# One burst on TensorE for the head outputs of a group, in place of two

## The reference, cut to what matters

```python
q, k, v = x @ Wq + bq, x @ Wk + bk, x @ Wv + bv      # per head, [8, 16, 512, 16]
scores = q @ k^T * 16 ** -0.5
probs = softmax(scores + causal mask)
y = probs @ v                                         # [8, 16, 512, 16]
x = layernorm(x + y @ Wo + bo)
f = silu(x @ fp8(gate_w) * gate_scale) * (x @ fp8(up_w) * up_scale)     # 768 wide
x = layernorm(x + f @ fp8(down_w) * down_scale)
```

## Time and profile before

| | |
|---|---|
| median of three runs | 589.0 us |
| the profiled execution | 590.27 us, of which the span is 588.5 us |
| TensorE clock over the span | 0.967 of full |

### The profile page before, as it was taken

The page is one execution under the profiler, slowest core; times in us unless marked ns, Lnnn a source line. Parts: engine busy times, 40 slices in busy tenths (PEclk is TensorE's granted clock), DMA queues, the critical chain, the costliest instruction groups (busy, mean ns, idle before and its releaser), DMA issues.

```text
span 588.5 us, 10775 instructions
## 1 busy us (share of the span) xinstructions
PE 539.8 (92%) x3968; PEld 357.9 (61%) x3968; DVE 443.7 (75%) x802; ACT 325.2 (55%) x578; POOL 220.3 (37%) x250
## 2 busy tenths in 40 slices
PE   4568699999999999999999999987899999999993
PEld 1333356656566556665665656654378888888883
DVE  4476567788788878888878888878545877778765
ACT  1206456666766667667666576664854544345430
POOL 3004332433344333443254334421335553455442
PEclk9858989999999999999999999999999999999998
DMA  6878846547446564744654744520000001110012
GB/s 158 224 220 247 231 125 163 170 138 196 150 111 195 148 164 148 183 149 144 144 184 125 200 146 125 155 51 3 2 1 0 8 31 36 37 37 16 22 36 73
DMA packets 62959, 69.07 MB, mean 117 GB/s; under 512 B 7418, under 2 KB 57210, under 8 KB 62906
## 3 DMA queue, kind: packets, MB, share of 16 engines
q1 hardware_dynamic: 62074, 67.85, 40.2%
q10 hardware_dynamic: 832, 0.53, 0.3%
HBM read 37.63 MB, written 29.62 MB: 114 GB/s over the span
## 4 chain that ended last, share of the span: by engine, by line
PE 79%; DVE 6%; DMA 5%; issue 4%; ACT 3%; SPq 1%; POOL 1%; ACTq 0%; POOLq 0%; DVEq 0%
PE ps L1008 13%; PE ps L893 12%; PE ps L885 12%; PE ps L804 10%; PE ps L812 9%; PE ps L1021 7%; PE ps L869 7%; PE ps L870 4%; DVE nmax L576 2%; DMA q_st<-zero_rows 2%; PE ps L835 2%; PE ps L828 2%; DMA m_scratch<-mrow 2%; PE ps L846 1%; DVE hT_l L641 1%
## 5 line engine op out<-in xcount | busy, mean ns | idle before, releaser
L576 DVE TENSOR_REDUCE nmax<-ps 128x2 f32<-128x1024 f32 (+1 forms) x192 | 196.9, 1041 | 76.3 <-PE ps L870 76.1
L421 ACT ACTIVATE probs<-ps 128x512 f32<-128x512 f32 x320 | 183.3, 594 | 80.8 <-PE ps L885 80.7
L346 POOL TENSOR_SCALAR_AFFINE_SELECT probs<-probs 128x512 f32<-128x512 f32 x128 | 86.6, 690 | 199.4 <-ACT probs L421 199.4
L885 PE MATMUL ps<-q_st,k_st 98*128 98x384 bf16 (+3 forms) x512 | 123.3, 304 | 5.4 <-ACT probs L421 3.2
L869 PE MATMUL ps<-k_st,q_st 98*128 98x256 bf16 (+2 forms) x384 | 85.1, 282 | 14.9 <-DMA q_st<-zero_rows 10.8
L374 POOL TENSOR_TENSOR f_l<-f_full,f_h 128x512 fp32r<-128x512 f32 x48 | 61.6, 1290 | 76.6 <-ACT f_h L494 76.6
L870 PE MATMUL ps<-k_st,q_st 124*128 124x128 bf16 x512 | 86.8, 226 | 0.0
L893 PE MATMUL ps<-probs,v_st 128*32 128x512 f32 (+3 forms) x1024 | 84.1, 447 | 0.2
L885 PEld LDWEIGHTS ps<-q_st,k_st 98*128 98x128 bf16 x512 | 44.1, 98 | 50.7 <-issue 27.1
L489 ACT ACTIVATE sgate<-ps,s_gate 128x512 f32<-128x512 f32 x48 | 32.9, 688 | 63.0 <-PE ps L1008 63.0
L869 PEld LDWEIGHTS ps<-k_st,q_st 98*128 98x128 bf16 x384 | 38.5, 100 | 36.3 <-issue 14.7
(11 more groups left out here) (85 smaller groups left out, 810.5 us busy)
## 6 DMA issues: line engine op xcount, KB each, us to landing
q_st<-q_scratch SPq DMA_DIRECT2D x32, 384.0 KB
k_st<-k_scratch SPq DMA_DIRECT2D x32, 384.0 KB
q_scratch<-part SPq DMA_DIRECT2D x16, 384.0 KB, 3.6
k_scratch<-part SPq DMA_DIRECT2D x16, 384.0 KB, 2.8
xT<-in_attn_xT SPq DMA_DIRECT2D x8, 512.0 KB, 3.9
q_scratch<-part SPq DMA_DIRECT2D x16, 256.0 KB, 3.7
k_scratch<-part SPq DMA_DIRECT2D x16, 256.0 KB, 2.0
resid<-in_attn_x SPq DMA_DIRECT2D x8, 512.0 KB, 3.8
```

Source lines behind the costliest of these rows:

```text
L346: pool.affine_select(out=blocks, in_=blocks, compare_op=ALU.is_ge, fill=0.0, base=0, pattern=[*pattern, [1, P]], channel_multiplier=-1).th ...
L421: act.activation(probs[:, u, :], ps[:, u % 2, :], ACT.Exp, scale=SCALE).then_inc(exp_done, 1)
L576: dve.tensor_reduce(nmax[:, i, heads[0]:heads[-1] + 1], src, AX.X, ALU.max, negate=True).then_inc(max_taken, 1)
L885: m = pe.matmul(ps[:, u % 2, c0:c0 + T - P * j], k_st[0:RP, g, h, P * j:P * j + P], q_st[0:RP, g, h, P * j:T], start=True, stop=True)
```

## The change

The four tiles of probabilities of the first key block get a second set of places: `probs` has 14 tiles in place of 10, and `slot(w, u)` chooses between two sets for u < 4 by the parity of w. `attend_first` and `attend_rest` become one `attend(w)`, which does all four key blocks in one sequence and stands where `attend_rest` stood: `attend(w - 1)` in group w, after scores piece 3. It waits for all the masks of its group. pv_done counts one per group in place of two. For the first exponential of group w, ScalarE now waits for attend(w - 2), and for the fifth for attend(w - 1).

The slots between the scores pieces are dealt out anew: scores_max piece 2 moves ahead of scores piece 6, the first half of the second projection moves behind scores piece 6, scores_max piece 3 moves ahead of scores piece 8, and the second half of that projection moves behind scores piece 8. ScalarE's, VectorE's, GpSimd's and SyncE's programs keep their order.

```diff
-    NU = 10
+    NU, NS = 10, 14
...
-        probs = carve(NU * T).rearrange("p (u t) -> p u t", u=NU)
+        probs = carve(NS * T).rearrange("p (u t) -> p u t", u=NS)
...
+        def slot(w, u):
+
+            return HG * (w % 2) + u if u < HG else HG + u
...
                 if u == 0:
-                    wait(act, pv_done, 2 * (w - 1) + 1)
+                    wait(act, pv_done, w - 1)
                 if u == HG:
-                    wait(act, pv_done, 2 * (w - 1) + 2)
-                act.activation(probs[:, u, :], ps[:, u % 2, :], ACT.Exp, scale=SCALE).then_inc(exp_done, 1)
+                    wait(act, pv_done, w)
+                act.activation(probs[:, slot(w, u), :], ps[:, u % 2, :], ACT.Exp, scale=SCALE).then_inc(exp_done, 1)
...
-            def attend_rest(w):
+            def attend(w):
...
                 pe.wait_ge(masked, 4 * w + 4)
-                attend(w, 1)
-                attend(w, 2)
-                attend(w, 3).then_inc(pv_done, 1)
+                for j in range(TB):
+                    for h in range(HG):
+                        u, c0 = prob_cols(w, j, h)
+                        m = pe.matmul(ps[HW * h:HW * h + HW, YB, P * j:T], v_st[:, (w // G) % 2, j, HG * g + h, :],
+                                      probs[:, u, c0:c0 + T - P * j], start=j == 0, stop=j == TB - 1)
+                m.then_inc(pv_done, 1)
...
                     scores(w, 5)
-                    work(n, g, 1, 0)
-                    scores(w, 6)
                     if more:
                         scores_max(w + 2, 2)
+                    scores(w, 6)
+                    work(n, g, 1, 0)
                     if w:
                         transpose_y(w - 1)
                     scores(w, 7)
-                    work(n, g, 1, 1)
-                    scores(w, 8)
                     if more:
                         scores_max(w + 2, 3)
+                    scores(w, 8)
+                    work(n, g, 1, 1)
                     scores(w, 9)
                     if more:
                         scores_max(w + 2, 4)
-                    attend_first(w)
```

More of the change, by code:

```diff
@@ L356, in _ @@
                     w, split = G * n + g, n + 1 < B and g in (0, 2)
-                    mask_units(w, 0, 3, probs[:, 0:HG, 0:P], [[0, HG]])
+                    first, later = probs[:, slot(w, 0):slot(w, 0) + HG], probs[:, 2 * HG:NS]
+                    mask_units(w, 0, 3, first[:, :, 0:P], [[0, HG]])
                     if split:
@@ L361, in _ @@
                         add_bias(n + 1)
-                    mask_units(w, 4, 7, probs[:, HG:2 * HG, 0:P], [[0, HG]])
-                    mask_units(w, 4, 7, probs[:, HG:2 * HG, 3 * P:T], [[0, HG]])
-                    mask_units(w, 8, 9, probs[:, 2 * HG:NU, :].rearrange("p u (v t) -> p (u v) t", v=2)[:, :, 0:P], [[0, HG]])
+                    mask_units(w, 4, 7, later[:, 0:HG, 0:P], [[0, HG]])
+                    mask_units(w, 4, 7, later[:, 0:HG, 3 * P:T], [[0, HG]])
+                    mask_units(w, 8, 9, later[:, HG:, :].rearrange("p u (v t) -> p (u v) t", v=2)[:, :, 0:P], [[0, HG]])
                     if split:
@@ L597, in empty_v @@
                 dve.wait_ge(v_full, n * 2 + v + 1)
-                wait(dve, pv_done, 2 * G * (n - 1))
+                wait(dve, pv_done, G * (n - 1))
                 dve.tensor_tensor(v_st[:, n % 2, 2 * v:2 * v + 2, :, 0:D],
@@ L887, in scores @@
                 m.then_inc(st_full, 1)
-            def attend(w, j):
+            def attend(w):
                 g = w % G
[L891 to L898, removed]
+                pe.wait_ge(masked, 4 * w + 4)
                 wait(pe, yn_ready, w)
                 pe.wait_ge(v_out, 2 * (w // G) + 2)
-                attend(w, 0).then_inc(pv_done, 1)
-            def attend_rest(w):
-                pe.wait_ge(masked, 4 * w + 4)
-                attend(w, 1)
-                attend(w, 2)
-                attend(w, 3).then_inc(pv_done, 1)
+                for j in range(TB):
[4 more added lines that the diff above has]
+                m.then_inc(pv_done, 1)
             def transpose_h(n, par, c, bank):
@@ L962, in _ @@
                     if w:
-                        attend_rest(w - 1)
+                        attend(w - 1)
                     scores(w, 4)
@@ L988, in _ @@
                         scores_max(w + 2, 5)
-            attend_rest(W - 1)
+            attend(W - 1)
             pe.wait_ge(quant, 8 * NQ)
```

9 lines of the change are left out of this document (5 added, 4 removed).

## The result

The changed kernel takes 601.35 us (median of four runs, 598.99 to 603.99), the kernel before beside it 590.32 us (four runs, 588.6 to 592.25). The ratio is 1.019, with a 95% interval of 1.016 to 1.023. The forecast was 593 us, with a range to 599 us: the sign was right, the size was not. It stood on a median of 589.0 us for the kernel before, which the fourth run raised by 1.3 us; against the kernel before it was +4.0 us, and +11.0 us were measured.

A forecast was written before the change was run, and what follows sets the result against it. TensorE's own instructions, one after the other, bound the steady part. Gain -6.2, costs +1.1, +4.1, +0.5, +2.2, +1.2, +0.4, +1.7 and start -0.6 sum to +4.4 us on 589.0: about 593 us, range 587 to 599.

The forecast's parts named there:

- The gain: Groups 2 to 29 on TensorE: joining two bursts into one saves 0.22 us a group, -6.2 us in all.
- the rival of a burst that doesn't get shorter: The join inside the burst costs 0.10 us, so the gain falls to 0.12 us a group: 596 us; chance 0.12.
- Cost 1: Scores piece 6 waits for ScalarE's exponential of piece 4: 0.04 us a group, +1.1 us over 28.
- Cost 2: Next group's first scores piece waits for ScalarE: 0.59 us after g=2 (+4.1 us), 0.09 us after g=0 (+0.5 us).
- Cost 3: Output projection after g=0 waits for ScalarE's copy of ynT 0.36 us more, six times: +2.2 us.
- Cost 4: VectorE takes the projection of v late after g=3: 0.13 us six times, plus 0.05 us seven times after g=2: +1.2 us.
- cost 5: Groups 30 and 31: exponentials and last burst come 0.88 us later, last burst 2.32 us for 1.44: +1.7 us.
- the start: First groups reach the transpose leading to a load TensorE waits for up to 1.2 us earlier: -0.6 us taken.
- The waits don't come: ScalarE reaches the exponential of piece 8 in time, costs 2 and 3 fall away (-6.8 us): 586.6 us; chance 0.15.
- VectorE falls behind: Late normalize_y and maxima push the transpose of the maxima out 0.3 us a group, 8.4 us: 601 us; chance 0.13.

The follow-up runs named there:

- e2: Changed kernel, one burst kept, with TensorE's slots put back in the order before the change: 608.34 us, 1.032 to the kernel before.
- e9: Kernel before, with its two bursts, given only the change's new slot order: 589.08 us, 0.998 to the kernel before.
- e3: Changed kernel with ScalarE taking the exponential of piece 8 ahead of the second projection's result (hi_part): 596.08 us, 1.011 to the kernel before.
- e4: Changed kernel plus 21 unread bf16 matmuls of 512 columns where TensorE waits in the last two groups: 597.29 us, 1.013 to the kernel before.
- e12: Changed kernel with one burst only in groups with g=1 and 3 up to 28, two in all others: 589.91 us, 1.002 to the kernel before.
- e15: Changed kernel with one burst only for g=1 and 3 up to group 28, two elsewhere, old slot order in the last three groups: 592.55 us, 1.003.

## Why the prediction was right in the mechanism and wrong in the size

**The gain held.** From scores piece 3 through the burst it is 2.62 us (220.26 to 222.88), where rows 3 gave 1.76 and 1.10 us with the gaps: 0.24 us a group, forecast 0.22. The burst of 2.30 us also refutes the rival of a burst that doesn't get shorter.

**Cost 1 held.** Scores piece 6 lost 0.04 us a group (212.86 where the matmul before it let it start at 212.82).

**Cost 2 held after g = 2** (0.67 us, forecast 0.59) and was undersized after g = 0: the scores piece came at 253.16 where 252.92 was free, 0.24 us for 0.09.

**Cost 3 held in kind.** The wait for ynT is 0.75 us (253.38 to 254.13) in place of 0.50, so 0.25 us more, forecast 0.36.

**Cost 4 was too small.** VectorE's late v_st cost 0.29 us in the sequence shown (241.07 to 241.36), against 0.13. The records of two other sequences show waits of 0.36 and 0.63 us. (The parts of this cost, 6 x 0.13 and 7 x 0.05 us, make 1.1 and not 1.2 us.)

Together, a sequence of four groups: -0.96 + 0.16 + 0.67 + 0.24 + 0.25 + 0.29 = +0.65 us. Measured is 48.32 - 47.65 = +0.67 us. The prediction's own signs came true: one burst of about 2.3 us, a wait of 0.4 to 0.6 us after g = 2, about half a us a sequence. The terms from the first output projection to the wait for h_in come to +4.3 us, forecast +3.3.

**The step that failed is cost 5, the end.** It said +1.7 us: 0.88 us for the later exponentials of group 31 and 0.88 us for the longer last burst. Measured are +7.6 us, in three parts. From scores piece 6 of group 30 to the feed-forward part there are four traces at full clock (1.00), one for each pair of burst and order:

| | two bursts | one burst |
|---|---|---|
| old slot order | 13.72 us (before) | 14.69 us (e2) |
| new slot order | 14.81 us (e9) | 15.78 us (e3) |

One burst costs 0.97 us in either order, and the new order 1.09 us with either burst. The changed kernel took 19.10 us, so 3.32 us more at its lower clock. From the wait for h_in to that scores piece it took 8.09 us against 5.88: 0.86 us for the longer burst (2.30 us for 1.44, both at full clock), and 1.35 us that its clock of 0.50 and 0.58 takes, beyond what the clock already took from the kernel before.

- The two terms that cost 5 named: 0.97 + 0.86 = 1.8 us, as forecast.
- The new slot order in these groups, where ScalarE is what TensorE waits for: 1.1 us. The prediction costed the order only for the steady part.
- The clock: 3.32 + 1.35 = 4.7 us in this trace. (The 4.95 us against e4 hold what the kernel before loses too; by the medians they are 4.1.) The prediction left it out. It took burst durations from the steady part, at full clock, and carried them into a stretch whose clock the trace of before already showed at 0.66.

Added up, the traces lie 12.8 us apart where 4.4 us were forecast. Of the 8.4 us between, 5.9 are this step, 1.0 the steady part, 0.2 the start, and 1.3 the feed-forward part, which differs as much between kernels that have it the same.

**The rivals.** "The waits don't come" fell by the seven waits of 0.51 us. Its price of 6.8 us, if ScalarE were in time, was too high as well: e3 puts the exponential first, and VectorE's `rest` takes ScalarE's place after g = 2, so that 0.5 us a sequence is gained. "VectorE falls behind" had the right time, 601 us, for a wrong reason: no transpose of the maxima is late in the changed kernel beyond 0.3 us. It named the engine that e2 shows as the next in line, and the changed kernel's new slot order exists to avoid it. That the VectorE chain was hidden by the burst was not in the prediction.

**What stays open.** Why VectorE is late with v_st in only some sequences of e12 and e15 is shown in part. In the late sequence of e15 the addition that writes v_st starts 2.00 us after the maximum of piece 3 does (330.68 to 332.68), in the one before 1.49 us (283.23 to 284.72). Between them one copy of the means took 0.36 us in place of 0.16 and waited 0.22 us, and the quantize step ahead of the maximum took 0.55 us in place of 0.35. Why the copy was slow is not shown. Nor is it shown what lets the clock fall before a burst: e3's last groups have the changed kernel's instructions and waits without the two later falls, and e4 shows that more work in the gaps keeps the clock up, no more. Its four runs lie within 0.9 us, the changed kernel's within 5.0 us.

## What to carry to other kernels

A short piece of work that looks like overhead can be the cover of two chains at once; before it is merged away, list for each engine what waits end while it runs, and cost the slot order that the merge will need. Cost the last iterations apart from the steady ones, with the clock that their own rows show: a longer piece behind a wait may be paid for at the lower clock, 3.9 us here in place of 2.3. When one wait is taken away, look for a second chain that ends at the same place, as after g = 2 in e3. And a gain of 0.24 us per iteration can be lost to an engine whose slack is below that, as to VectorE in e15.

## What the hardware showed

- The same burst took 2.30 us from start to next start in the steady part and 3.88 us (416.11 to 419.99) at a mean granted clock of 0.58 (0.50 up to 418.00, 0.66 from there): 1.7 times.
- 21 dummy matmuls in TensorE's idle places made the kernel 4.1 us faster by the medians (601.35 to 597.29 us), and all three bursts ran at full clock.
- The same instructions with the same waits took 23.38 us in one execution (e3) and 27.19 us in another, with one slow burst in the first and three in the second.
- A matmul that waits for ScalarE started 0.73 us after ScalarE's exponential of 0.59 us did (228.22 to 228.95), 0.09 us more than in the earlier trace rows; so chains worked out from one such pair are good to about 0.1 us, which over 28 groups is 2.8 us.
